# A mixture-of-experts stage with its small projection halves packed into one tile, its routing a tile earlier, and its lead-in maxima placed anew

## What is computed

```python
scores = jax.nn.softmax(xf @ gate_w.T, axis=-1)
biased = scores + gate_b
_, idx = lax.top_k(biased, K)                                   # K = 2
w = jnp.take_along_axis(scores, idx, axis=-1) * ROUTER_SCALE
rw = jnp.zeros((T, E)).at[jnp.arange(T)[:, None], idx].add(w)
h = silu((einsum('td,edh->teh', xf, w1) + b1) * (einsum('td,edh->teh', xf, w3) + b3))
y = einsum('te,ted->td', rw, einsum('teh,ehd->ted', h, w2) + b2)
z = silu((xf @ sw1 + sb1) * (xf @ sw3 + sb3)) @ sw2 + sb2       # the shared expert
return (y + z).reshape(shape)
```

## Time and profile before

| | |
|---|---|
| median of three runs | 1060.96 us (1057.96 to 1062.22) |
| the profiled execution | 1063.57 us, span 1061.8 us |
| busy in the span: PE, DVE, ACT, POOL | 947.9, 783.9, 753.1, 536.7 us |
| expert stage | about 335 to 619 us of the span |
| attention of layer 1 | 619 to about 1010 us |

### The profile page before, as it was taken

The page is one execution under the profiler, slowest core; times in us unless marked ns, Lnnn a source line. Parts: engine busy times, 40 slices in busy tenths (PEclk is TensorE's granted clock), DMA queues, the critical chain, the costliest instruction groups (busy, mean ns, idle before and its releaser), DMA issues. The chain is left out here.

```text
span 1061.8 us, 23047 instructions
## 1 busy us (share of the span) xinstructions
PE 947.9 (89%) x8688; PEld 519.1 (49%) x8688; DVE 783.9 (74%) x1324; ACT 753.1 (71%) x1380; POOL 536.7 (51%) x748
## 2 busy tenths in 40 slices
PE   5788789889898999999999989999999999899896
PEld 3333334333344888888877733333333333333564
DVE  4777767778792676766677768888898888895465
ACT  2477677778776666566555469888888888888663
POOL 3465655675553022213210148785867778666344
PEclk8699999999999999999999989999999999999999
DMA  6323412211202733333322110212112020200011
GB/s 177 110 82 87 136 51 86 79 50 41 84 15 55 186 93 101 90 91 109 111 83 87 52 52 30 75 32 64 31 54 73 14 74 26 70 11 16 23 31 50
DMA packets 63582, 73.91 MB, mean 70 GB/s; under 512 B 14120, under 2 KB 45992, under 8 KB 63088
## 3 DMA queue, kind: packets, MB, share of 16 engines
q1 hardware_dynamic: 62608, 71.66, 23.4%
q10 hardware_dynamic: 864, 0.79, 0.4%
HBM read 39.24 MB, written 2.77 MB: 40 GB/s over the span
## 5 line engine op out<-in xcount | busy, mean ns | idle before, releaser
L862 ACT ACTIVATE at_E<-at_Sb 128x512 f32<-128x512 f32 x832 | 445.6, 599 | 81.2 <-PE at_Sb L715 75.7
L926 DVE TENSOR_REDUCE mx<-at_Mb 128x2 f32<-128x1024 f32 x242 | 281.9, 1217 | 43.0 <-PE at_Mb L678 41.8
L763 PE MATMUL at_Ob<-at_E,VP 128*32 128x256 f32 (+2 forms) x2816 | 213.9, 377 | 16.6 <-ACT Oev L890 10.4
L715 PE MATMUL at_Sb<-QP,KP 64*128 64x512 bf16 (+3 forms) x1024 | 204.5, 347 | 10.4 <-ACT full_k L417 3.6
L1028 POOL TENSOR_TENSOR at_E<-at_E,factor 128x512 f32<-128x512 f32 x128 | 162.4, 1273 | 76.8 <-ACT at_E L862 66.8
L678 PE MATMUL at_Mb<-KP,QP 62*128 62x512 bf16 x996 | 174.5, 356 | 18.0 <-DVE mx L926 15.4
L929 DVE TENSOR_REDUCE mx<-at_Mb 128x2 f32<-128x768 f32 (+1 forms) x128 | 138.4, 1087 | 57.0 <-PE at_Mb L678 55.7
L1039 POOL TENSOR_SCALAR_AFFINE_SELECT at_E<-at_E 128x512 f32<-128x512 f32 x128 | 82.7, 659 | 76.4 <-ACT at_E L862 76.4
L763 PEld LDWEIGHTS at_Ob<-at_E,VP 128*32 128x32 f32 x2816 | 57.1, 108 | 119.7 <-issue 88.1
L715 PEld LDWEIGHTS at_Sb<-QP,KP 64*128 64x128 bf16 x1024 | 74.9, 96 | 72.3 <-ACT at_E L862 36.1
L1468 DVE TENSOR_TENSOR ex_hh<-ex_R,ex_th 128x512 f32<-128x512 f32 x88 | 64.5, 733 | 60.1 <-ACT ex_th L1406 59.4
(11 more groups left out here) (207 smaller groups left out, 1446.2 us busy)
## 6 DMA issues: line engine op xcount, KB each, us to landing
QP<-q SPq DMA_DIRECT2D x96, 128.0 KB, 2.4
KP<-k SPq DMA_DIRECT2D x90, 128.0 KB, 2.4
ex_R<-rw_dram SPq DMA_DIRECT2D x32, 256.0 KB, 3.9
ctxN<-Oev SPq DMA_DIRECT2D x16, 256.0 KB, 3.0
denB<-rdram SPq DMA_DIRECT2D x64, 64.0 KB
ex_R<-rw_dram SPq DMA_DIRECT2D x16, 224.0 KB, 4.1
ex_R<-rw_dram SPq DMA_DIRECT2D x16, 192.0 KB, 3.6
ex_R<-rw_dram SPq DMA_DIRECT2D x16, 160.0 KB, 3.5
```

Of the source, the lines that this page charges most:

```text
L715: return pe.matmul(out[:, at:at + SEQ - q0], KP[p0:p0 + ROWS_H, b % 2, 2 * g + a, kt * P:(kt + 1) * P], QP[p0:p0 + ROWS_H, b % 2, 2 * g + ...
L763: last = pe.matmul(Ob[VW * i:VW * (i + 1), 0, q0:q1], weights_of(b, G, kt, i, q0), moving, start=(kt == 0 and q0 == 0), stop=False, skip_g ...
L862: nc.scalar.activation(dst, src, ACT.Exp).then_inc(s["s_read"], 1)
L926: v.tensor_reduce(mx[:, G % 2, :, t % 2, t // 2], src, AX.X, ALU.max).then_inc(s["m_read"], 1)
```

## The change

1. **Shared tile 1.** The 48 columns of w1 and the 48 of w3 stand in one tile of the w1 array (columns 0 to 47 and 64 to 111), so TensorE runs three matmuls for tile 1, all into `Ab`. ScalarE copies rows 64 to 111 of `Ab` to rows 0 to 47 of `up3`, and VectorE's product works on 48 rows.
2. **Routing** a tile earlier: logits at tile 4, shift and exponential at 5, softmax at 6, top-2 at 7, weights at 8. The transpose of the weights stays at 10.
3. **Lead-in maxima.** `LEAD_AT` is a new list, and the maximum is taken in the tile after its scores, between that tile's product and its hidden product.
4. **Last update.** The last gated sum goes to `ctxT` in place of `t1`, and GpSimd adds it to `x` at beat 0 of the next stage. VectorE waits for it ahead of its first context product there.

```diff
-LEAD_AT = sorted({(5, 4), (5, 11), (6, 3), (6, 4), (6, 10), (6, 12), (7, 1), (7, 2), (7, 4), (7, 5), (7, 7), (7, 8), (7, 10), (7, 11)})
+LEAD_AT = [(5, 4), (5, 9), (5, 11), (6, 1), (6, 3), (6, 9), (6, 11), (7, 0), (7, 2), (7, 5), (7, 7), (7, 9), (7, 10), (7, 11)]
...
+                if not causal and (n, at) == (1, CTX_AT):
+                    v.wait_ge(ex["xup"], NBATCH)
...
+                if not causal and beat == 0:
+                    xb = sb["x"][:, last_b * SEQ:]
+                    p.wait_ge(ex["t1"], NBATCH)
+                    p.tensor_tensor(xb, xb, sb["ctxT"][:], ALU.add).then_inc(ex["xup"], 1)
...
-            update_x(last_b)
...
+                if j == 1:
+                    rows = slice(RW_AT, RW_AT + HID_END)
+                    nc.scalar.activation(up3[0:HID_END, q, :], Ab[rows, q, :], ACT.Identity, bias=b3[rows, j:j + 1])\
+                      .then_inc(s["u3"], 1)
+                    return
...
-                        if j == 6:
+                        if j == 5:
                             route_exp(nc, a, sb, s, b + 1)
...
-                v.scalar_tensor_tensor(z[:, q, :], Ab[:, q, :], b1[:, j:j + 1], up3[:, q, :],
+                rows = HID_END if j == 1 else P
+                v.scalar_tensor_tensor(z[0:rows, q, :], Ab[0:rows, q, :], b1[0:rows, j:j + 1], up3[0:rows, q, :],
                                        ALU.add, ALU.mult).then_inc(s["z"], 1)
...
-                        if j == 6:
+                        if j == 5:
                             route_shift(v, sb, s, b + 1, logits_of(b + 1))
                             v.sem_inc(s["free"], 1)
+                        if j == 6:
+                            route_softmax(v, sb, s, b + 1)
                         if j == 7:
-                            route_softmax(v, sb, s, b + 1)
+                            route_top(v, sb, s, b + 1)
                         if j == 8:
-                            route_top(v, sb, s, b + 1)
-                        if j == 9:
                             route_weights(v, sb, s, b + 1)
+                    lead = divmod(N * b + j - 1, N)
+                    if lead in LEAD_AT:
+                        lead_reduce(v, sb, nx, LEAD_AT.index(lead), Fb[:])
                     if j >= SHARED:
                         hidden(b, j, half)
-                    if (b, j) in LEAD_AT:
-                        lead_reduce(v, sb, nx, LEAD_AT.index((b, j)), Fb[:])
...
-            gated(last_b)
+            gated(last_b, sb["ctxT"])
...
-                for bankk, w in ((Ab, "w1"), (Bb, "w3")):
+                for bankk, w in ((Ab, "w1"), (Bb, "w3"))[0:1 if j == 1 else 2]:
...
-                        if j == 5:
+                        if j == 4:
                             logits(b + 1)
```

More of the change, by code:

```diff
@@ L1469, in hidden, with gated @@
                  .then_inc(s["hh"], 1)
-            def gated(b):
+            def gated(b, t1):
                 v.wait_ge(s["y"], b + 1)
@@ L1482, in body @@
                     if j == 1 and not is_int(b, 0):
-                        gated(b - 1)
+                        gated(b - 1, t1)
                     if is_int(b, 0) and j == 1:
@@ L2007, in layout @@
     d["gate_b"] = f(np.asarray(i["L0_ffn_gate_b"])[None])
-    pad = SHARED * P - HID
     for n in ("1", "3"):
         up = np.asarray(i[f"L0_ffn_w{n}"]).transpose(1, 0, 2).reshape(D, EXPERTS * HID)
-        d[f"w{n}"] = f(np.concatenate([np.pad(np.asarray(i[f"L0_ffn_sw{n}"]), ((0, 0), (0, pad))), up], 1))
-        bb = np.concatenate([np.pad(np.asarray(i[f"L0_ffn_sb{n}"]), (0, pad)), np.asarray(i[f"L0_ffn_b{n}"]).reshape(-1)])
+        shared, sb = np.zeros((D, SHARED * P), np.float32), np.zeros(SHARED * P, np.float32)
+        shared[:, 0:P], sb[0:P] = np.asarray(i[f"L0_ffn_sw{n}"])[:, 0:P], np.asarray(i[f"L0_ffn_sb{n}"])[0:P]
+        at = P if n == "1" else P + RW_AT
+        sb[at:at + HID_END] = np.asarray(i[f"L0_ffn_sb{n}"])[P:]
+        if n == "1":
+            shared[:, P:HID] = np.asarray(i["L0_ffn_sw1"])[:, P:]
+            shared[:, P + RW_AT:P + RW_AT + HID_END] = np.asarray(i["L0_ffn_sw3"])[:, P:]
+        d[f"w{n}"] = f(np.concatenate([shared, up], 1))
+        bb = np.concatenate([sb, np.asarray(i[f"L0_ffn_b{n}"]).reshape(-1)])
         d[f"b{n}"] = f(bb.reshape(HTILES, P).T)
```

## The result

| | kernel before | changed kernel |
|---|---|---|
| median of 20 runs each, taken in turn | 1064.2 us (1057.96 to 1069.25) | 1055.34 us (1048.9 to 1060.52) |
| ratio, 95% interval | | 0.992 (0.9904 to 0.9936) |
| span of the profiled execution | 1061.8 us | 1047.2 us |
| first up projection to first score matmul of the next stage | 335.36 to 619.00, 283.64 us | 330.57 to 605.65, 275.08 us |

The changed kernel is faster by 8.9 us, 0.8%. Forecast were 8.6 us and 1052.3 us. The difference was met; the absolute time is 3 us above the forecast, because the 20 runs of before have a median 3.2 us above that of the first three, from which the forecast was subtracted.

A forecast was written before the change was run, and what follows sets the result against it. TensorE, busy 267 of 284 us in the expert stage, was taken as the bound. Packing 3.8, routing 4.6, maxima -1.1 and last update 1.3 sum to 8.6 us off the 1060.96 median: 1052.3 us, range 1047.5 to 1058.

The forecast's parts named there:

- The new wait behind the gated sum: First down projection after the packed tile waits about 0.26 us in batches 1, 2, 3 and 5, leaving 0.43 of 0.69.
- VectorE gets ahead by about 0.1 us only: At a batch's start, packing lets VectorE's gated sum come only about 0.1 us earlier, so 0.26 us of wait appears.
- in 4, 6 and 7 extra matmuls stand between and the full 0.69 stays: In batches 4, 6 and 7, transposes or lead-in scores precede the down projection, so packing keeps 0.69 us each.
- The fear behind the lower bound: Routing's bound of 2 us: the wait for the table loads grows by 0.4 us a batch.
- The rule: Lead-in maxima: read at 4.31 us, next pair at 4.37; neighbours 2.0 us late, pairs two tiles apart just in time.
- the one at tile 3 of batch 6: Score pair there 0.8 us late, because the normalisation stands ahead of the maximum on VectorE.
- Rival (b): Clock falls to 1.2 GHz at tiles 10 and 11 of the last batch: 3.3 us, 1055.6 us; chance 0.12.
- what is left of the stage: From the last batch's tiles 10 and 11 on, the lower clock would cost 3.3 us over the stage's remainder.
- If the clock shows under 1.00 before the last gated sum (then (b)): Sign in the trace after: a clock under 1.00 ahead of the last gated sum would make the clock rival right.
- (a): VectorE and ScalarE set the pace at a batch's start; packing only moves the wait: gain 4.8, 1056 us; chance 0.18.
- (c): Pairs two tiles behind the last one also wait 1.3 to 2.0 us: 10.5 us more, 1062.8 us; chance 0.07.
- (d): The new placement of maxima costs nothing: 13.6 us gained, 1047.4 us; chance 0.08.

The follow-up runs named there:

- e9: Kernel before with the packed tile and the new placement of lead-in maxima only: stage 281.08 us against 283.64, ratio 0.9975.
- e1: Kernel before with the packed shared tile alone: stage 281.98 us against 283.64, ratio 1.0006.
- e3: Kernel before with the new list of lead-in pairs and the maximum in the next tile alone: stage 284.11 us against 283.64, ratio 1.0006.
- e7: Changed kernel with VectorE's gated sum ahead of tile 1's product: stage 274.29 us, ratio to the kernel before 0.9928.
- e10: Changed kernel with the gated sum ahead of tile 1's product and the normalisation in tile 1: stage 272.33 us, ratio to the kernel before 0.9889.
- e5: Changed kernel with one pair moved from batch 7, tile 10, to batch 5, tile 2, so none are neighbours: stage 270.33 us, ratio to before 0.9873.
- the second trace: The changed kernel run again with nothing altered: stage 275.26 us, ratio to the kernel before 0.993.
- e6_same_tile: Changed kernel with its new list, but the maximum behind the hidden product of the same tile: stage 274.12 us, ratio to the kernel before 0.9921.
- e4_last_only: Kernel before with the last update in the next stage alone: stage 282.20 us against 283.64, ratio 0.9985.

## Why the prediction was right, and where it was not

**The difference.** 8.6 us forecast, 8.56 and 8.38 measured in the stage, 8.9 (7 to 10) by time. That it came so close is partly luck: packing alone was 2.1 us less than its term, routing and maxima 0.65 and 0.63 better than theirs, and packing and maxima help each other by 1.37, which no term had.

| term | forecast | alone on the kernel before |
|---|---|---|
| packing | 3.8 | 1.66 (3.03 beside the new list) |
| routing | 4.6 | 5.25 |
| maxima | -1.1 | -0.47 |
| last update | 1.3 | 1.44 |
| sum | 8.6 | 7.88, and 1.37 more by packing and maxima together |

**Packing.** Mechanism right, size wrong. The new wait behind the gated sum is there in batches 1, 2, 3 and 5, with 0.37 us in tile 2 instead of 0.26: "VectorE gets ahead by about 0.1 us only" was too kind to it. Batch 0 lost a little instead of nothing. The step that failed is "in 4, 6 and 7 extra matmuls stand between and the full 0.69 stays": for batches 6 and 7 it held only where no maximum stands ahead of the product of tile 0. It is true of the changed kernel (by e9) and false of the kernel before (by e1). The forecast took this part's worth for a property of the part, and only the list beside it made it so.

**Routing.** The wait for the weights went, and the wait for the table loads moved to tile 7 with 0.43 us as before: both as forecast. Mis-sized were batch 0 (0.63 instead of 0.1) and batch 4 (1.80 instead of 1.38), against 0.03 to 0.13 too much in each of batches 1, 2, 3 and 5. The fear behind the lower bound, that the wait for the table loads would grow, fell. In the changed kernel, where the switches run beside another tile, the loads are 1.28 us again, ScalarE's gaps ahead of and behind each of them are 0.01 to 0.02 us, and the wait behind both is the same 0.43. The Trainium skill (ScalarE: Activation LUTs, "What ACT_TABLE_LOAD costs") gives each switch 1.38 us of drain beside the load; no drain shows here, and the measurement decides.

**Maxima.** The rule (read at 4.31, next pair at 4.37 from the tile's start; neighbours 2.0 us late, pairs two tiles apart just in time) held in every kernel with this order: at full clock 1.8 us by the matmul rows and 2.0 by the weight loads' for neighbours, nothing for pairs two tiles apart, that of tile 3 in batch 6 aside. Of the small waits, the one at tile 3 of batch 6 was counted at 0.8 and has 0.4 (3.2 us in the list of waits, less 1.81 and 0.99). The term came out at -0.47, not -1.1, and this holds a fall of the clock of some 0.6 us, which the term had left out; without it the new placement would have cost nothing.

**Rival (b), the clock.** It stood with 0.12 and half of it came true. The clock fell to the lower of its two levels (1.2 GHz; 0.57 is the mean of a window that holds some of the full rate too) behind the first or the second wait in all six traces of kernels with neighbouring pairs and the later maximum (e3, e7, e9, e10 and the changed kernel twice). In the seven other traces it didn't fall between batch 1 and the stage's last down projection. But it came back to 1.00 after 3.4 us, so it cost 0.4 and 1.0 us in the changed kernel (0.2 in e7) and not the 3.3 worked out for "what is left of the stage". One premise was read wrong: the idle time of 1.25 us stands in tile 4 of batch 6, and batch 7 had at most 1.11 for a pair. "If the clock shows under 1.00 before the last gated sum (then (b))" was the wrong sign: it told the mechanism, not the price. The Trainium skill (TensorE: Matmul & The Clock Gate, Part 1) has an idle TensorE put to half rate. The traces agree in kind: each of these falls comes behind a tile in which TensorE idled 1.8 us of 4.7.

**The other rivals.** (a) fell as it was put: tile 2 gives back 0.37 of 0.69 in batches 1, 2, 3 and 5, not all; beside the old list it comes near to true in batches 6 and 7 (0.11 gained and 0.14 lost by e1). (c) fell with e5. (d) fell: the neighbours wait in every kernel that has them, and e5 shows that 4.9 us lie in them, clock included.

**Last update.** 1.44 us instead of 1.3; TensorE was back 0.33 us behind the sum, where 0.35 had been named. What the clock does at the head of the next stage was in no term.

**Signs by batch.** Batches 1 to 3 were to be near 32.2 and are 32.36, batch 6 near 34.7 and is 34.26; batch 7 was to be no shorter and is 0.56 shorter.

**What the sum still lacks.** The four parts with the interaction of 1.37 would give 9.25 us; all together gave 8.38 and 8.56. Batch by batch the traces account for it. In batch 5 the parts alone add up to 1.21 us and the changed kernel gains 0.85: the new list has a pair at the end of tile 9 there, and with it tile 10 takes 3.02 us in e3 already, 3.53 before, so routing finds less of its wait left (2.73 in the second trace). That is 0.36. The clock makes up nearly all the rest: against the fall that e3 holds, the second trace loses 0.45 more at the end, and the first 0.46 in batch 0 and 0.17 less at the end.

**What stays open.** Why the clock falls behind the first wait in some traces and behind the second in others, and why the packing makes batch 0 0.29 us longer.

## What to carry to other kernels

Where two engines hand over a single buffer, work out for each place when the reader is done and when the writer is due, in the unit of one tile: here that gave 2.0 us for neighbours and nothing for every second tile, and moving one pair of fourteen was worth as much as half of the whole change. A step that shortens one engine's row pays only if nothing else on its chain is queued behind something: price it in each neighbourhood that it will stand in, that of the changed kernel too. Where the gain is in tenths per batch, read the stage and not the span, since unchanged code ahead of it varies by more, and read it batch by batch with the granted clock beside it, since two traces can agree in the sum by differences that cancel.

## What was not expected of the hardware

Where TensorE waited 1.8 us in a tile with a neighbouring pair and was busy for the rest of it, its clock came down to half, behind the first such wait (594.4 us in the first trace) or behind the second (599.4 in the other), in six traces of six; idle times of 1.11 us (batch 7) and 1.25 us (batch 6) in the kernel before left it at 1.00, and so did the 1.47 us ahead of its last down projection. It was back at the full rate 3.4 us after each of these falls.

At the start of the stage, behind the barrier, it fell in two traces of thirteen (331.6 us in the changed kernel's first, 334.3 in e6_same_tile), with the same 1.27 us of idle time ahead of the first matmul in both traces of the changed kernel. So the same work gets either clock there, at a price of 0.4 to 0.5 us. Over the gap between the two stages (1.14 us idle of TensorE's matmuls at 605.65) the clock stays at 1.00 in the changed kernel, and falls only some microseconds into the next stage:

```profile
605.65:608.00 2.35, 1.90 (x11) 0.82 (x11) 1.93 (x2) 2.34 (x4) 1.25 (x1) 1.00 0.01 3
608.00:615.00 7.00, 6.57 (x19) 1.49 (x19) 4.04 (x4) 5.76 (x12) 2.73 (x5) 0.51 0.00 0
```

The start of the expert stage differs by up to 8.5 us between traces of kernels whose code ahead of it is the same, and what follows the stage by up to 7 us (441.6 us behind it in the changed kernel's first trace, 448.6 in e4_last_only), while batches 1 to 3 of the stage repeat within 0.04 us in the same kernel.
